# Two k products run together chunk by chunk, with the last maxima rounds between the chunks

## The chip, the cores and the metric

The kernel runs on one core of one Trainium2 chip. Everything is measured in microseconds of device time, from the start to the end of one execution. TensorE, VectorE (DVE), ScalarE (ACT), GpSimd (POOL) and SyncE (SP, which only issues transfers here) run their own instruction streams, and semaphores tie them together.

## What is computed

The input x holds 4 sequences of 2048 tokens of 512 numbers, the context 4 times 154 tokens. A layer norm, a cross attention and a gated channel mix (FFN) follow each other; cut to what matters:

```
xn = layernorm(x)
Q, K, V = xn @ Wq.T, ctx @ Wk.T, ctx @ Wv.T          # 16 heads of 32
x = x + tanh(g_xattn) * (softmax(Q K.T / sqrt(32)) V) @ Wo.T
x2 = layernorm(x)
xr = mu_r * x2 + (1 - mu_r) * x2_prev                # x2_prev: the token before
xk = mu_k * x2 + (1 - mu_k) * x2_prev
k = relu(xk @ W_k.T) ** 2
out = x + tanh(g_ffn) * sigmoid(xr @ W_r.T) * (k @ W_v.T)
```

## The kernel before

The 8192 tokens go in 16 blocks of 512. A product of two float32 matrices is made of three matmuls (high by high, high by low, low by high part), so one 128 x 512 piece of a product over 512 inputs takes 4 chunks of 3 matmuls. The step of block i (the function `step`, written once for each engine) computes the attention of block i and, between its parts, the FFN of block i - 1 and the queries of block i + 1. Step 0 has no FFN and transposes weights in its place; steps 1 to 14 are one hardware loop, step 15 and an epilogue with the last block's FFN stand behind it. So the FFN stands beside attention in fifteen steps.

The order on every engine is written out by hand, and each engine works strictly through its own list. What matters for the change is the start of a step:

- VectorE mixes the rows of k into the banks `o_bank` and `d_bank` (`mix_k`, line 865), ScalarE takes their high part (line 492) and VectorE their low part (`xk_low`, line 722). TensorE's k products (`ffn_k`, line 1176) wait for these low parts chunk by chunk. Output chunks 0 and 2 of k go to `g_bank` 0, chunks 1 and 3 to `g_bank` 1.
- Of the maxima of the scores (`maxima` on TensorE, line 1080; `reduce_max` on VectorE, line 813), there are six rounds. Rounds 0 to 3 lie in the step before. Round 4 has twelve small matmuls and four reduces, round 5 four and four. A round's matmuls wait for the reduces of the round before, as both use the four `s_bank`s.
- The maxima are transposed into `o_bank` (`maxima_transposed`, line 1007), and ScalarE copies them (`mT_copy`, line 492). The head scores of group 0 (`head_scores`, lines 1104 and 1108) need that copy for their last four matmuls. The next mixing for r (`mix_r(1)`, line 875) also waits for it, since it writes the same bank.
- Then ScalarE takes two exponentials from each bank (lines 598 and 599), VectorE the low half of the first (`p_low`, line 817), and the tail scores (`tail_scores`, line 1114) wait for that one, since they go to `s_bank` 0 again.
- VectorE takes the relu of each k chunk out of its bank (`k_relu`, line 842). GpSimd squares it (line 425), ScalarE and GpSimd split it (lines 492 and 429). k products 2 and 3 wait for the relus of 0 and 1, which free their banks. k product 1 waits for the copy of the fourth query out of `g_bank` 1 (`q_copy`, line 582).

In the kernel before, TensorE's list reads: k0 with round 4 ahead of its chunk 2; k1 with round 5 ahead of its chunk 1; the transpose of the maxima; k2 with the head scores ahead of its chunk 2; the tail scores; k3 and the first r product. VectorE's list behind the mixing reads: reduces of round 4, relu 0, reduces of round 5, relu 1, then `mix_r(1)`, `xr_low(0)`, `mix_r(2)`, `xr_low(1)`, `p_low(0)`.

Of the kernel before, what the change touches and what calls it, by code (L numbers as in the profile page):

```python
# [14 lines left out]
PRODUCTS = ((HI, HI), (HI, LO), (LO, HI))  # L15


def flamingo_block(nc, x, ctx_tokens, g_xattn, g_ffn, Wq, Wk, Wv, Wo, W_r, W_k, W_v, mu_r, mu_k, out):
# [8 lines left out]
    C = D // P  # L27
# [3 lines left out]
    BLOCKS = B * T // N  # L31
# [15 lines left out]
    with ExitStack() as ctx:  # L47
# [9 lines left out]
        WqT, WoT, WrT, WkT2, WvT2 = (sb(n, [P, 2, C, D], F32R) for n in ("WqT", "WoT", "WrT", "WkT2", "WvT2"))  # L57
# [6 lines left out]
        buf3 = sb("buf3", [P, 2, C, N], F32R)  # L64
# [107 lines left out]
        K_BANK = [g_bank[n] for n in (0, 1, 0, 1)]  # L172
# [547 lines left out]
        def _(dve):  # L720
# [115 lines left out]
            def k_relu(i, c):  # L836
                dve.wait_ge(k_done, i * C + c + 1)
                if c >= 2:
                    dve.wait_ge(k2_lo, i * C + c - 1)
                else:  # L840
                    later(dve, k2_lo, i * C)
                nc.vector.tensor_scalar(k2[c % 2], K_BANK[c][:, :], 0.0, None, ALU.max).then_inc(relu_ready, 1)  # L842
# [51 lines left out]

            def step(i, ffn, pre):
                reduce_max(i, 4)
                if ffn:
                    k_relu(i - 1, 0)
                else:
                    weight_low(late_units(0))  # L900
                reduce_max(i, 5)
                if ffn:
                    k_relu(i - 1, 1)
                    mix_r(i - 1, 1)
                    xr_low(i - 1, 0)
                    mix_r(i - 1, 2)
                    xr_low(i - 1, 1)
                p_low(i, 0, 0)
                if ffn:
                    mix_r(i - 1, 3)  # L910
                    xr_low(i - 1, 2)
                p_low(i, 0, 1)
                if ffn:
                    k_relu(i - 1, 2)
                    xr_low(i - 1, 3)
                p_low(i, 0, 2)
                p_low(i, 0, 3)
                if ffn:
                    k_relu(i - 1, 3)
                p_low(i, 0, 4)  # L920
                if not ffn:
                    weight_low(late_units(1))
                if pre:
                    moments1(i + 1, 0)
                    moments1(i + 1, 1)
                for g in range(1, G):
                    attend(i, g - 1)
                    p_low(i, g, 0)
                    p_low(i, g, 1)
                    if ffn and g == 2:  # L930
                        gated(i - 1, 1, pre)
                    if pre and g == 3:
                        xT_low(i + 1, 0)
                    p_low(i, g, 2)
                    p_low(i, g, 3)
                    p_low(i, g, 4)
                    if ffn and g != 2:
                        gated(i - 1, g - 1, pre)
                    if not ffn:
                        weight_low(late_units(1 + g))  # L940
                    if pre and g == 1:
                        moments1(i + 1, 2)
                        moments1(i + 1, 3)
                if pre:
                    for t in range(1, TT):
                        xT_low(i + 1, t)
                if not ffn:
                    weight_low(late_units(1 + G))
                attend(i, G - 1)
                if pre:  # L950
                    reduce_max(i + 1, 0)
                    reduce_max(i + 1, 1)
                    reduce_max(i + 1, 2)
                elif ffn:
                    gated(i - 1, TT - 1, pre)
                residual(i, 0, pre)
                if pre:
                    reduce_max(i + 1, 3, (0, 1))
                residual(i, 1, pre)
                if pre:  # L960
                    reduce_max(i + 1, 3, (2, 3))
                residual(i, 2, pre)
                residual(i, 3, pre)
                if pre and ffn:
                    gated(i - 1, TT - 1, pre)
                mix_k(i, 0)
                mix_k(i, 1)
                xk_low(i, 0)
                mix_k(i, 2)
                xk_low(i, 1)  # L970
                mix_k(i, 3)
                xk_low(i, 2)
                keep_carry(i)
                xk_low(i, 3)
                mix_r(i, 0)
# [19 lines left out]
        def _(pe):  # L995
# [14 lines left out]
            def cols(n):  # L1010
                return slice(P * n, P * n + P)
# [57 lines left out]
            def maxima(i, r):  # L1069

                if r == 0:
                    pe.wait_ge(k_loaded, 16 * K_LOADS * (i + 1))
                    later(pe, p_lo, i * SCORE_UNITS)
                    pe.wait_ge(xT_lo, (i + 1) * TT)
                else:
                    pe.wait_ge(reduced, i * MAX_UNITS + 4 * r)
                pe.wait_ge(q_hi, i * G + ROUNDS[r][-1][0] + 1)
                for n, (g, t) in enumerate(ROUNDS[r]):
                    for j in range(4):
                        ins = nc.tensor.matmul(s_bank[j][:, S * n:S * n + S], buf4[rows(j), HI, g, cols(t)], k_all[rows(j), g, :],  # L1080
                                               start=True, stop=True)
                        if n == len(ROUNDS[r]) - 1:
                            ins.then_inc(max_done, 1)
# [7 lines left out]
            def maxima_transposed(i):  # L1091
                pe.wait_ge(reduced, (i + 1) * MAX_UNITS)
                later(pe, x2_ready, i * TT - 1)
                transposed(mT_bank, [mm[:, t, :] for t in range(TT)]).then_inc(mT_done, 1)

            def head_scores(i, g):

                if g:
                    pe.wait_ge(p_lo, i * SCORE_UNITS + 5 * g)
                pe.wait_ge(q_lo, i * G + g + 1)  # L1100
                for k, (s, q) in enumerate(PRODUCTS):
                    for j in range(4):
                        keys = k_all[rows(j), g, 0:P] if s == HI else k_low[rows(j), g, :]
                        nc.tensor.matmul(s_bank[j][:, :], keys, buf4[rows(j), q, g, :], start=k == 0, stop=False)  # L1104
                if g == 0:
                    pe.wait_ge(mT_ready, i + 1)
                for j in range(4):
                    nc.tensor.matmul(s_bank[j][:, :], negsel[rows(j), g, DH * j:DH * j + 1].to_broadcast([DH, P]), mT[rows(j), :],  # L1108
                                     start=False, stop=True).then_inc(scores_done, 1)
# [51 lines left out]
                    pe.wait_ge(x2_ready, i * TT + t - 1)  # L1161
                transposed(x2_bank[t], [xn2[t % 2][:, cols(c)] for c in range(C)]).then_inc(x2_done, 1)

            def ffn_k(i, c, queries=True, before=None):


                if c >= 2:
                    pe.wait_ge(relu_ready, i * C + c - 1)
                elif c == 1 and queries:
                    pe.wait_ge(q_copied, (i + 1) * G + 4)  # L1170
                for e in range(C):
                    if before:
                        before(e)
                    pe.wait_ge(xk_lo, i * C + e + 1)
                    for n, (s, m) in enumerate(PRODUCTS):
                        ins = nc.tensor.matmul(K_BANK[c][:, :], WkT2[:, s, e, cols(c)], buf3[:, m, e, :],  # L1176
                                               start=(e, n) == (0, 0), stop=(e, n) == (C - 1, len(PRODUCTS) - 1))
                ins.then_inc(k_done, 1)

            def ffn_r(i, t):  # L1180

# [19 lines left out]
            def at(chunk, what):  # L1201
                return lambda c: what() if c == chunk else None
# [11 lines left out]

            def step(i, ffn, pre):
                if ffn:
                    ffn_k(i - 1, 0, before=at(2, lambda: maxima(i, 4)))
                    ffn_k(i - 1, 1, before=at(1, lambda: maxima(i, 5)))
                    maxima_transposed(i)
                    ffn_k(i - 1, 2, before=at(2, lambda: head_scores(i, 0)))  # L1220
                else:
                    maxima(i, 4)
                    weights_transposed(late_units(0))
                    maxima(i, 5)
                    maxima_transposed(i)
                    head_scores(i, 0)
                tail_scores(i, 0)
                if ffn:
                    ffn_k(i - 1, 3)
                    ffn_r(i - 1, 0)  # L1230
                else:
                    weights_transposed(late_units(1))
# [73 lines left out]
                step(i, True, True)  # L1306
            step(BLOCKS - 1, True, False)
            pe.wait_ge(x1_ready, BLOCKS * TT)
            for c in range(C):
                ffn_k(BLOCKS - 1, c, queries=False)  # L1310
            for t in (0, 1):
                ffn_r(BLOCKS - 1, t)
            for t in (0, 1):
# [25 lines left out]
```

## Time and profile before

| what | us |
|---|---|
| median of 3 runs (1563.97 to 1566.31) | 1564.04 |
| the profiled execution's own time | 1564.87 |
| its span, from the first to the last instruction | 1563.0 |
| TensorE busy (92%) | 1431.4 |
| VectorE busy (69%) | 1082.3 |
| ScalarE busy (50%) | 777.8 |
| GpSimd busy (39%) | 612.4 |
| mean granted TensorE clock | 0.951 |

Busy time is a sum of instruction times. The ends of matmuls are modelled and overlap the next one's start, so the distance from start to start is the better measure of a matmul's price. The granted clock is 1.00 for 2.4 GHz and 0.50 for 1.2 GHz. In a timeline an entry "x9" merges nine instructions; the bracket at its end tells how long the engine stood still before it and what ended that.

### The profile page before, as it was taken

What the parts mean: (1) busy time and instruction counts of PE and PEld (TensorE: products, weight loads), DVE (VectorE), ACT (ScalarE), POOL (GpSimd) and SP (SyncE); (2) the same over time, 40 slices, a digit from 0 to 9 for tenths busy, and PEclk for the clock granted to TensorE, in tenths of its full rate; (3) what the DMA queues carried; (4) which work ended last, traced back from release to release, by engine and by line L of the source; (5) the groups of instructions that cost most, each with busy time, mean ns of one, the idle gap of its engine ahead of it and who ended that gap; (6) DMA issues with size and microseconds to landing.
All of it is one profiled execution on the core that took longest, in us unless ns stands there. A gap on an engine that the chain in (4) does not pass through costs nothing.

```text
span 1563.0 us, 28266 instructions
## 1 busy us (share of the span) xinstructions
PE 1431.4 (92%) x9616; PEld 1041.5 (67%) x9616; DVE 1082.3 (69%) x1926; ACT 777.8 (50%) x1412; POOL 612.4 (39%) x807
## 2 busy tenths in 40 slices
PE   7866899998989899898989989898989989898978
PEld 6744667676767667676666757676766767666656
DVE  3465676867677686767777686767768676777652
ACT  3355273644637364554636455463736455463631
POOL 1111343535344442534344352534445253434333
PEclk9968899999999999998999999999999999999989
DMA  4422011121202012121101112120111212110100
GB/s 155 141 81 74 28 48 41 54 60 47 67 27 62 25 60 53 47 67 44 55 28 60 40 54 60 47 67 27 57 30 54 60 47 67 38 61 22 41 21 34
DMA packets 98364, 84.09 MB, mean 54 GB/s; under 512 B 49440, under 2 KB 62752, under 8 KB 98336
## 3 DMA queue, kind: packets, MB, share of 16 engines
q1 hardware_dynamic: 98336, 83.72, 17.9%
q8 instruction: 17, 0.28, 0.1%
q14 instruction: 11, 0.09, 0.0%
HBM read 58.79 MB, written 20.71 MB: 51 GB/s over the span
## 4 chain that ended last, share of the span: by engine, by line
PE 81%; DVE 10%; ACT 3%; issue 2%; POOL 1%; DMA 1%; SPq 1%; DVEq 0%; POOLq 0%; ACTq 0%
PE g_bank L1001 45%; PE g_bank L1176 9%; PE o_bank L1130 6%; PE s_bank L1104 4%; PE d_bank L1136 4%; PE s_bank L1114 3%; PE s_bank L1080 3%; DVE buf L722 2%; DVE o_bank L865 2%; PE o_bank L1007 2%; PE s_bank L1001 2%; DVE d_bank L865 2%; DVE mm L813 2%; PE d_bank L1007 1%; PE s_bank L1007 1%
## 5 line engine op out<-in xcount | busy, mean ns | idle before, releaser
L1176 PE MATMUL g_bank<-buf,WkT 128*128 128x512 f32 x768 | 236.1, 456 | 68.9 <-DVE buf L722 66.4
L813 DVE TENSOR_REDUCE mm<-s_bank 128x3 f32<-128x462 f32 (+1 forms) x384 | 198.7, 577 | 103.2 <-PE s_bank L1080 103.2
L817 DVE TENSOR_TENSOR pq<-s_bank,pq 128x512 f16<-128x512 f32 x320 | 218.4, 687 | 61.6 <-ACT s_bank L599 61.3
L598 ACT ACTIVATE pq<-s_bank 128x512 f16<-128x512 f32 x320 | 192.7, 602 | 108.1 <-PE s_bank L1108 108.0
L1176 PEld LDWEIGHTS g_bank<-buf,WkT 128*128 128x128 f32 x768 | 157.1, 217 | 123.6 <-DVE buf L722 76.8
L1001 PE MATMUL g_bank<-xnT,WqT 128*128 128x512 f32 x768 | 200.0, 407 | 3.6 <-DVE xnT L801 2.1
L599 ACT ACTIVATE s_bank<-s_bank 128x512 f32<-128x512 f32 x320 | 195.1, 610 | 0.0
L1001 PE MATMUL g_bank<-WvT,buf 128*128 128x512 f32 x768 | 192.3, 397 | 0.0
L1001 PE MATMUL g_bank<-WoT,buf 128*128 128x512 f32 x768 | 189.9, 397 | 0.0
L1001 PE MATMUL g_bank<-WrT,buf 128*128 128x512 f32 x768 | 188.9, 395 | 0.0
L433 POOL TENSOR_TENSOR buf<-place,buf 128x512 fp32r<-128x512 f32 x64 | 82.4, 1288 | 255.6 <-ACT buf L492 255.6
L1001 PEld LDWEIGHTS g_bank<-xnT,WqT 128*128 128x128 f32 x768 | 142.6, 192 | 40.5 <-DVE xnT L801 8.2
L1001 PEld LDWEIGHTS g_bank<-WrT,buf 128*128 128x128 f32 x768 | 141.8, 188 | 40.2 <-issue 11.0
L1001 PEld LDWEIGHTS g_bank<-WvT,buf 128*128 128x128 f32 x768 | 140.9, 188 | 34.2 <-issue 5.8
L1001 PEld LDWEIGHTS g_bank<-WoT,buf 128*128 128x128 f32 x768 | 140.7, 188 | 30.5
L429 POOL TENSOR_TENSOR buf<-place,buf 128x512 fp32r<-128x512 f32 x64 | 83.3, 1301 | 105.4 <-ACT buf L492 105.4
L492 ACT ACTIVATE buf<-place 128x512 fp32r<-128x512 f32 x128 | 81.4, 636 | 81.0 <-DVE place L834 65.8
L421 POOL TENSOR_TENSOR buf<-xa,buf 128x512 fp32r<-128x512 f32 x64 | 83.5, 1304 | 92.0 <-ACT xa L582 92.0
L441 POOL TENSOR_TENSOR x<-place,x 128x512 f32<-128x512 f32 x48 | 61.7, 1286 | 127.7 <-DVE place L847 127.7
L400 POOL TENSOR_TENSOR ve<-mv,eps 128x1 f32<-128x1 f32 x128 | 24.3, 190 | 216.3 <-DVE mv L767 216.3
L563 ACT ACTIVATE xa<-x,nb,rstd 128x512 f32<-128x512 f32 x64 | 52.0, 813 | 107.1 <-POOL nb L404 105.3
L425 POOL TENSOR_TENSOR place<-place 128x512 f32<-128x512 f32 x64 | 73.3, 1145 | 76.5 <-DVE place L842 76.5
(125 smaller groups left out, 2179.9 us busy)
## 6 DMA issues: line engine op xcount, KB each, us to landing
xa<-in_x SPq DMA_DIRECT2D x64, 256.0 KB, 2.7
x<-in_x SPq DMA_DIRECT2D x64, 256.0 KB, 2.7
out<-x SPq DMA_DIRECT2D x48, 256.0 KB, 2.0
k_all<-k_scratch SPq DMA_DIRECT2D x16, 256.0 KB, 2.8
k_low<-k_scratch SPq DMA_DIRECT2D x16, 256.0 KB, 2.9
v_main<-v_scratch SPq DMA_DIRECT2D x16, 256.0 KB, 2.8
place<-x SPq DMA_DIRECT2D x16, 256.0 KB, 2.3
out<-place SPq DMA_DIRECT2D x16, 256.0 KB, 2.0
```

Of the source, the lines that this page charges most:

```text
L421: nc.gpsimd.tensor_tensor(buf4[:, LO, g, :], q32[g], buf4[:, HI, g, :].bitcast(F32), ALU.subtract).then_inc(q_lo, 1)
L425: nc.gpsimd.tensor_tensor(k2[c % 2], k2[c % 2], k2[c % 2], ALU.mult).then_inc(k2_ready, 1)
L429: nc.gpsimd.tensor_tensor(buf1[:, LO, c, :], k2[c % 2], buf1[:, HI, c, :].bitcast(F32), ALU.subtract).then_inc(k2_lo, 1)
L433: nc.gpsimd.tensor_tensor(buf3[:, LO, g, :], attn32, buf3[:, HI, g, :].bitcast(F32), ALU.subtract).then_inc(attn_lo, 1)
L492: nc.scalar.activation(dst, src, ACT.Copy).then_inc(done, 1)
L598: nc.scalar.activation(pq[:, n, HI, :], bank[:, :], ACT.Exp, scale=SCALE).then_inc(p_hi, 1)
L599: nc.scalar.activation(bank[:, :], bank[:, :], ACT.Exp, scale=SCALE).then_inc(p_full, 1)
L813: nc.vector.reduce_max(maxima, scores, AX.X).then_inc(reduced, 1)
L817: nc.vector.tensor_tensor(pq[:, n, LO, :], score_bank[5 * g + n][:, :], pq[:, n, HI, :], ALU.subtract).then_inc(p_lo, 1)
L1001: ins = nc.tensor.matmul(dst, stationary(s, c), moving(m, c), start=(c, n) == (0, 0), stop=(c, n) == (chunks - 1, len(PRODUCTS) - 1))
L1130: nc.tensor.matmul(o_bank[rows(j), :], v, pq[:, 4 if n else j, q, :], start=(n, k) == (0, 0), stop=(n, k) == (1, 2))
L1176: ins = nc.tensor.matmul(K_BANK[c][:, :], WkT2[:, s, e, cols(c)], buf3[:, m, e, :], start=(e, n) == (0, 0), stop=(e, n) == (C - 1, len(PRO ...
```

## The change

TensorE now runs k0 and k1 together: for each of the four chunks of the mixed rows, three matmuls for output chunk 0 and three for output chunk 1. Round 4's maxima stand ahead of chunk 1 of this pair, round 5's ahead of chunk 3. The wait for the fourth query's copy, which stood ahead of k1, stands ahead of the pair. k2 follows, with the transpose of the maxima ahead of its chunk 2, then the head scores, and behind them directly the tail scores. On VectorE the relu of chunk 0 moves behind the reduces of round 5, so that both relus stand there. The epilogue takes the pair, k2 and k3 in the same way.

```diff
--- before.py
+++ after.py
@@ -894,12 +894,11 @@
 
             def step(i, ffn, pre):
                 reduce_max(i, 4)
-                if ffn:
-                    k_relu(i - 1, 0)
-                else:
+                if not ffn:
                     weight_low(late_units(0))
                 reduce_max(i, 5)
                 if ffn:
+                    k_relu(i - 1, 0)
                     k_relu(i - 1, 1)
                     mix_r(i - 1, 1)
                     xr_low(i - 1, 0)
@@ -1161,21 +1160,23 @@
                     pe.wait_ge(x2_ready, i * TT + t - 1)
                 transposed(x2_bank[t], [xn2[t % 2][:, cols(c)] for c in range(C)]).then_inc(x2_done, 1)
 
-            def ffn_k(i, c, queries=True, before=None):
-
-
-                if c >= 2:
-                    pe.wait_ge(relu_ready, i * C + c - 1)
-                elif c == 1 and queries:
+            def ffn_k(i, columns, queries=True, before=None):
+
+
+                if columns != (0, 1):
+                    pe.wait_ge(relu_ready, i * C + columns[0] - 1)
+                elif queries:
                     pe.wait_ge(q_copied, (i + 1) * G + 4)
                 for e in range(C):
                     if before:
                         before(e)
                     pe.wait_ge(xk_lo, i * C + e + 1)
-                    for n, (s, m) in enumerate(PRODUCTS):
-                        ins = nc.tensor.matmul(K_BANK[c][:, :], WkT2[:, s, e, cols(c)], buf3[:, m, e, :],
-                                               start=(e, n) == (0, 0), stop=(e, n) == (C - 1, len(PRODUCTS) - 1))
-                ins.then_inc(k_done, 1)
+                    for c in columns:
+                        for n, (s, m) in enumerate(PRODUCTS):
+                            ins = nc.tensor.matmul(K_BANK[c][:, :], WkT2[:, s, e, cols(c)], buf3[:, m, e, :],
+                                                   start=(e, n) == (0, 0), stop=(e, n) == (C - 1, len(PRODUCTS) - 1))
+                        if e == C - 1:
+                            ins.then_inc(k_done, 1)
 
             def ffn_r(i, t):
 
@@ -1214,10 +1215,9 @@
 
             def step(i, ffn, pre):
                 if ffn:
-                    ffn_k(i - 1, 0, before=at(2, lambda: maxima(i, 4)))
-                    ffn_k(i - 1, 1, before=at(1, lambda: maxima(i, 5)))
-                    maxima_transposed(i)
-                    ffn_k(i - 1, 2, before=at(2, lambda: head_scores(i, 0)))
+                    ffn_k(i - 1, (0, 1), before=lambda e: maxima(i, {1: 4, 3: 5}[e]) if e % 2 else None)
+                    ffn_k(i - 1, (2,), before=at(2, lambda: maxima_transposed(i)))
+                    head_scores(i, 0)
                 else:
                     maxima(i, 4)
                     weights_transposed(late_units(0))
@@ -1226,7 +1226,7 @@
                     head_scores(i, 0)
                 tail_scores(i, 0)
                 if ffn:
-                    ffn_k(i - 1, 3)
+                    ffn_k(i - 1, (3,))
                     ffn_r(i - 1, 0)
                 else:
                     weights_transposed(late_units(1))
@@ -1306,8 +1306,9 @@
                 step(i, True, True)
             step(BLOCKS - 1, True, False)
             pe.wait_ge(x1_ready, BLOCKS * TT)
-            for c in range(C):
-                ffn_k(BLOCKS - 1, c, queries=False)
+            ffn_k(BLOCKS - 1, (0, 1), queries=False)
+            ffn_k(BLOCKS - 1, (2,))
+            ffn_k(BLOCKS - 1, (3,))
             for t in (0, 1):
                 ffn_r(BLOCKS - 1, t)
             for t in (0, 1):
```

## Rows read from the trace of the kernel before

**Rows 1.** The page's part 1, and its part 4, the chain that ended last.
```profile
PE 1431.4 (92%) x9616; PEld 1041.5 (67%) x9616; DVE 1082.3 (69%) x1926; ACT 777.8 (50%) x1412; POOL 612.4 (39%) x807
...
PE 81%; DVE 10%; ACT 3%; issue 2%; POOL 1%; DMA 1%; SPq 1%; DVEq 0%; POOLq 0%; ACTq 0%
```

**Rows 2.** Waits: who waited for whom; us in total, times, longest.
```profile
PE g_bank L1176 <- DVE buf L722: 66.4, 18, 5.5
...
PE s_bank L1114 <- DVE pq L817: 12.6, 18, 2.8
...
PE s_bank L1080 <- DVE mm L813: 8.8, 9, 2.4
```

**Rows 3.** Timeline, TensorE: start, us, engine, line, operation, tiles, count, wait before.
```profile
454.60 3.10 PE L1176 MATMUL g_bank<-buf,WkT 128*128 128x512 f32 x6 [4.00 <-DVE buf L722]
...
461.88 0.34 PE L1080 MATMUL s_bank<-k_all,buf 32*128 32x154 f32 x4 [1.28 <-DVE mm L813]
462.15 2.34 PE L1176 MATMUL g_bank<-buf,WkT 128*128 128x512 f32 x9
464.33 0.60 PE L1007 MATMUL o_bank<-ident,mm 128*128 128x128 f32 x4
464.68 1.64 PE L1176 MATMUL g_bank<-buf,WkT 128*128 128x512 f32 x6
466.26 0.73 PE L1104 MATMUL s_bank<-buf,k_all 32*128 32x512 f32 x8
...
467.38 1.66 PE L1176 MATMUL g_bank<-buf,WkT 128*128 128x512 f32 x6
469.44 0.96 PE L1114 MATMUL s_bank<-buf,k_tail 128*128 128x512 f32 x3 [0.40 <-DVE pq L817]
```

**Rows 4.** Timeline of the same stretch, VectorE.
```profile
459.55 2.27 DVE L813 TENSOR_REDUCE mm<-s_bank 128x3 f32<-128x462 f32 x4
461.74 0.68 DVE L842 TENSOR_SCALAR place<-g_bank 128x512 f32<-128x512 f32 x1
462.34 0.98 DVE L813 TENSOR_REDUCE mm<-s_bank 128x1 f32<-128x154 f32 x4
...
465.60 0.76 DVE L875 SCALAR_TENSOR_TENSOR o_bank<-place,mu,x 128x512 f32<-128x512 f32 x1 [0.38 <-ACT mT L492]
...
468.70 0.68 DVE L817 TENSOR_TENSOR pq<-s_bank,pq 128x512 f16<-128x512 f32 x1
```

**Rows 5.** Timeline of the same stretch, ScalarE and GpSimd.
```profile
454.48 0.59 ACT L582 ACTIVATE xa<-g_bank 128x512 f32<-128x512 f32 x1
...
464.97 0.60 ACT L492 ACTIVATE mT<-o_bank 128x512 fp32r<-128x512 f32 x1 [4.69 <-PE o_bank L1007]
...
468.06 0.59 ACT L599 ACTIVATE s_bank<-s_bank 128x512 f32<-128x512 f32 x1
...
462.50 1.04 POOL L425 TENSOR_TENSOR place<-place 128x512 f32<-128x512 f32 x1 [4.27 <-DVE place L842]
```

**Rows 6.** Timeline, TensorE, in a block whose k products start at 722.60.
```profile
725.64 0.93 PE L1080 MATMUL s_bank<-k_all,buf 32*128 32x154 f32 x12
726.49 4.21 PE L1176 MATMUL g_bank<-buf,WkT 128*128 128x512 f32 x9
730.63 0.50 PE L1080 MATMUL s_bank<-k_all,buf 32*128 32x154 f32 x4
```

**Rows 7.** Windows: us, busy (count) of PE, PEld, DVE, ACT, POOL, clock, DMA, GB/s.
```profile
454.60:457.90 3.30, 3.30 (x10) 1.93 (x14) 3.15 (x5) 1.67 (x3) 2.99 (x3) 0.50 0.00 0
...
123.50:126.80 3.30, 3.23 (x11) 2.74 (x12) 2.02 (x4) 3.30 (x8) 1.28 (x1) 0.50 0.00 0
```

**Rows 8.** Timeline, TensorE, in the block before the loop and at the end.
```profile
123.56 1.65 PE L1114 MATMUL s_bank<-buf,k_tail 128*128 128x512 f32 x3 [2.06 <-DVE pq L817]
...
1529.21 7.36 PE L1176 MATMUL g_bank<-buf,WkT 128*128 128x512 f32 x24 [2.45 <-DVE place L842]
1536.41 5.60 PE L1001 MATMUL g_bank<-WrT,buf 128*128 128x512 f32 x24
```

## The prediction

> **What bounds the kernel now.** I read four views. The page's shares come first: TensorE is busy 92% of the span and holds 81% of the chain that ended last [rows 1]. So a change pays only where TensorE stands still or runs at its low clock. The sums of waits come second: TensorE's largest wait is for the mixed rows of k (66.4 us in 18 waits). Its second is for the low half of the first exponentials ahead of the tail scores (12.6 us in 18) [rows 2]. The third view is the order of time in one block. All fifteen blocks with an FFN part repeat it about 89.3 us apart (454.60, 543.94, and so on), and the change works in it. The fourth is the granted clock. The sum is made against the profiled execution, 1564.87 us (span 1563.0); the median of the runs is 0.83 lower.
>
> Take the block whose k products start at 454.60 after 4.00 us of standing still [rows 3]; times below count from there. TensorE does k0's first two chunks, the maxima of round 4, k0's rest and k1's first chunk. Then it waits 1.28 us until VectorE has reduced round 4, and does round 5 at 7.28. That start is VectorE's: its four reduces run 459.55 to 461.82 [rows 4], right behind its mixing. It is the same to 0.03 us in eleven of the fifteen blocks; in one it is 6.91, and in three where the low clock lasts it is 8.03 (as 722.60 to 730.63) [rows 6]. Then come the rest of k1 (nine matmuls, 2.18 us), the transpose of the maxima at 9.73, six matmuls of k2, the head scores (from 11.66 to 12.78), the last six matmuls of k2, and the tail scores at 14.84 after a wait of 0.40. The tail scores wait for VectorE's 0.68 at 468.70 to 469.38. This has two roads. ScalarE's second exponential ends at 468.65 [rows 5], 2.4 after the head scores began. VectorE can begin its own row only after mix_r(1) at 465.60, which waited for ScalarE's copy of the transposed maxima (464.97), and three operations behind it. Both roads begin at the transpose, and the tail scores come 5.11 us after it. **So the time of the transpose, not the amount of matmuls, sets the end of this stretch.**
>
> **The change, part by part.** No instruction is added or removed; matmuls, reduces and relus are as many as before. No DMA is issued or moved, and SP's queue keeps its order. What moves is TensorE's order and one relu on VectorE.
>
> *Start of the pair.* The wait for the fourth query copy stood ahead of k1 and now stands ahead of the first chunk. That copy ends at 455.07 (454.48 and 0.59) [rows 5], so the pair starts 0.47 late. This is covered: up to round 5 TensorE now has 18 matmuls and the twelve of round 4. At the high clock that is 18 times 0.242 (2.18 over nine) and 0.5, 4.9 us; from 0.47 it ends at 5.3, before the 7.28 that VectorE sets. At the low clock a matmul takes 0.46 (nine from 726.49 to 730.63) and the maxima 0.85 [rows 6]: 9.1 us, ending at 9.6. The clock is at half in the first 3.3 us of this block, [rows 7], and in the one of 722.60 nine of its matmuls still run at the slow pace [rows 6]. So the cost lies between 0 and 2.3 us a block; but before, too, the slow blocks lost 0.75 here, and the new order leaves fewer holes. I take 0.1.
>
> *Relus behind round 5.* Round 5 starts at 7.28 as now. VectorE is free, so it starts reducing some 0.3 later and is done with its 0.98 [rows 4] at 8.6. k0 ends at 8.43 (round 5's matmuls 0.27, three matmuls 0.73, and the 0.15 by which the last one's end trails), so relu 0 starts at about 8.6. From a relu's start to its waiter's there is 0.76 (461.74 to GpSimd's 462.50) [rows 4, 5]. So k2 starts at 9.33, where TensorE is through with k1 at 9.0: a new wait of 0.3. Bounds: none, if relu 0 were early, and 0.75 if nothing of it hid.
>
> *Transpose behind k2's first half.* Six matmuls, 1.45 us, bring it to 10.78. Before it was 9.73: **1.05 us later in each block**. Without the new wait it would be 0.72, with the whole 0.75 it would be 1.5. The Trainium skill (TensorE: Matmul & The Clock Gate, "Back-to-back issue gap") gives 216 ns a matmul of 512 columns at full clock. By it the six take 1.30 and the nine of before 1.94, which makes the difference 1.14; the trace has 242 ns, and the sum goes by that.
>
> *Head to tail.* The transpose's 0.35, six matmuls (1.58 up to the next, as 464.68 to 466.26) put the head scores 1.93 behind the transpose, exactly as before. They take 1.12. The tail scores stay 5.11 behind the transpose, so the wait ahead of them grows from 0.40 to 2.06, as the six matmuls that covered it are gone. Behind this wait stand k3, r0 and the first values, with all their readers, so it moves everything by 1.05. Nothing later takes that back: besides the two waits named, only the one for round 4's reduce recurs among TensorE's own (8.8 us in nine) [rows 2], and the next block's mixing is fed by TensorE's own transposes. GpSimd's square of k0 moves from 462.50 to about 464.0 and ends 1.04 later; it is needed once ScalarE has copied the maxima, about 1.5 us later. If that cover were gone the exponentials would queue behind it. The low part and chunks 2 and 3 of the relus shift with the rest.
>
> *Epilogue.* At 1529.21 k2 waits for relu 0 already [rows 8], which stands on VectorE behind seven operations of mixing in both orders: nothing.
>
> *The clock in the new wait.* The block before the loop has no k2 to cover the same place: the tail scores follow the head scores directly and start at 123.56 after a wait of 2.06, and from 123.5 to 126.8 the clock is 0.50, 1.2 instead of 2.4 GHz [rows 7, 8]. A wait of 2.45 at the end has the same consequence: 24 matmuls take 7.36 instead of 5.60 us, 1.76 more [rows 8]. Waits of 1.28 [rows 3] keep the clock high. The new wait is 2.06. The low stretches begin at varying places of the waits, so I do not take a fall in every block: bounds 0 and 15, taken 6, costing 10.5.
>
> Sum: 15 x (1.05 + 0.1) = 17.3, and 10.5: 1564.9 + 27.8 - 0.8 = 1591.9; I say 1591. The forecast's own range is 1585 to 1600 (3 to 10 falls).
>
> **Rivals.** *No falls:* what speaks for it is that every wait of a full TensorE under 1.3 us keeps the clock, and that tail scores and k3 follow densely. 1581.
>
> *Falls in every block:* every wait of 2 us and more that I found is followed by a low stretch. 17.3 + 26.4: 1608.
>
> *No change:* the shift is used up later in the block, at a place where TensorE waits for VectorE or ScalarE anyway and so would start when it starts now. It decides if such a wait of 1 us stands behind the tail scores; the sums show none that recurs [rows 2]. 1564, within 0.2%.
>
> *Faster:* the transpose is not what the tail scores hang on. If VectorE's mixing behind the copy left the first low half at its old distance from round 5, the path would be TensorE's own matmuls, and these have become shorter behind round 5: six instead of nine, 0.73 a block, 11 us in all, 1553. It decides when the wait ahead of the tail scores stays at 0.4. The 5.11 us that repeat in every block speak against it.
>
> *Evacuation:* the Trainium skill (Perfetto Trace Analysis, "Matmuls") wants independent groups in turn through the banks, so that one is emptied under the next one's matmuls. Here both banks are full at once, and the 0.3 is what that costs; it is in the sum.
>
> **How the numbers follow.** Forecast 0.56, no falls 0.30, falls everywhere 0.06, no change 0.04, faster 0.04. About 0.2% (3 us) can be told from no change. So slower 0.92, same 0.04, faster 0.04. The range reaches from the no-falls case with the smaller bound (15 x 0.85, 1577) up to 1603, some twelve falls. It leaves out the two small cases and the far end of the falls.
>
> **What would show it.** Round 5's maxima still 7.3 after the old start of k (6.8 after the new one); a wait of 0.3 ahead of k2 for a relu; the transpose 3.5 instead of 2.45 behind round 5; a wait of about 2 us ahead of the tail scores in each block, some followed by clock 0.50; total of that wait near 40 us. The prediction is wrong if that wait stays under 1 us, if the transpose comes no later, or if round 5 starts over 1 us late since the clock stays low.

## The result and the profile after

| | us |
|---|---|
| before, median of 4 runs (1563.97 to 1566.31) | 1565.11 |
| after, median of 4 runs (1593.67 to 1599.06) | 1597.03 |
| ratio, 95% interval | 1.0202 [1.0179, 1.0224] |
| the profiled execution after | 1599.06, span 1597.3 |

The change makes the kernel 2% slower, some 32 us. A second set of four runs of it, beside the last experiments, gave 1595.88 and 1.0207 [1.0188, 1.0227]. The profiled execution is 34.2 us longer than that of before, and this is the difference that I take apart below. (The forecast started from 1564.04, the median of the three runs known then.)

The page of the changed kernel, the same two lines as in [rows 1]:

```profile
PE 1434.9 (90%) x9616; PEld 1047.9 (66%) x9616; DVE 1084.6 (68%) x1926; ACT 776.3 (49%) x1412; POOL 612.4 (38%) x807
...
PE 80%; DVE 10%; ACT 4%; issue 3%; POOL 2%; SPq 1%; DMA 1%; DVEq 0%; POOLq 0%; ACTq 0%
```

TensorE has 3.5 us more of busy time and 34 us more of span. These sums do not price the clock. Matmuls at the low clock count as busy, and where TensorE would otherwise wait for VectorE the low clock costs nothing. In the kernel before, the blocks that start at 454.60 and 543.94 are 89.34 and 89.33 us long. The first is at the low clock until 3.4 behind its start and then waits 1.28 ahead of round 5. The second is at the low clock until 6.2 and waits 0.01. So the loss has to be read block by block. TensorE's own waits, the counterparts of [rows 2]:

```profile
PE g_bank L1176 <- ACT xa L582: 69.1, 15, 4.6
PE s_bank L1113 <- DVE pq L817: 35.6, 18, 2.1
...
PE s_bank L1079 <- DVE mm L813: 3.7, 6, 2.4
```

The wait ahead of the tail scores (L1113, L1114 before) grew from 12.6 to 35.6 us, by 23. The wait for the mixed rows at the start of k now ends with ScalarE's copy of the fourth query (L582). It is 4.61 in each block but the last (4.52) instead of 4.00: the copy ends at 737.15, and the pair starts 0.15 later.

One block in order of time, TensorE, the counterpart of [rows 3], with ScalarE's copy ahead of it. Its k products start at 737.30:

```profile
736.56 0.59 ACT L582 ACTIVATE xa<-g_bank 128x512 f32<-128x512 f32 x1
...
737.30 2.92 PE L1176 MATMUL g_bank<-buf,WkT 128*128 128x512 f32 x6 [4.61 <-ACT xa L582]
...
740.72 3.01 PE L1176 MATMUL g_bank<-buf,WkT 128*128 128x512 f32 x12
743.96 0.34 PE L1079 MATMUL s_bank<-k_all,buf 32*128 32x154 f32 x4 [0.23 <-DVE mm L813]
744.23 3.40 PE L1176 MATMUL g_bank<-buf,WkT 128*128 128x512 f32 x12
747.47 0.60 PE L1006 MATMUL o_bank<-ident,mm 128*128 128x128 f32 x4
747.83 1.64 PE L1176 MATMUL g_bank<-buf,WkT 128*128 128x512 f32 x6
749.40 0.74 PE L1103 MATMUL s_bank<-buf,k_all 32*128 32x512 f32 x8
...
750.20 0.39 PE L1107 MATMUL s_bank<-mT,negsel 32*128 32x512 f32 x4
752.58 0.97 PE L1113 MATMUL s_bank<-buf,k_tail 128*128 128x512 f32 x3 [1.99 <-DVE pq L817]
...
753.62 4.51 PE L1176 MATMUL g_bank<-buf,WkT 128*128 128x512 f32 x12
757.97 2.91 PE L1000 MATMUL g_bank<-WrT,buf 128*128 128x512 f32 x12
```

And VectorE in the same block, as in [rows 4]:

```profile
741.64 2.27 DVE L813 TENSOR_REDUCE mm<-s_bank 128x3 f32<-128x462 f32 x4
744.33 0.99 DVE L813 TENSOR_REDUCE mm<-s_bank 128x1 f32<-128x154 f32 x4 [0.43 <-PE s_bank L1079]
745.24 1.36 DVE L842 TENSOR_SCALAR place<-g_bank 128x512 f32<-128x512 f32 x2
748.74 0.76 DVE L875 SCALAR_TENSOR_TENSOR o_bank<-place,mu,x 128x512 f32<-128x512 f32 x1 [2.14 <-ACT mT L492]
...
751.85 0.68 DVE L817 TENSOR_TENSOR pq<-s_bank,pq 128x512 f16<-128x512 f32 x1
```

The new start of k lies 0.61 later than the old one against the mixing, so 0.61 is added to set these times beside the old ones ("on the old scale"). Round 5 is at 6.66 (7.27 on the old scale, 7.28 before). Behind it twelve matmuls take 3.24 instead of the 2.91 that twelve cost at 0.242: that includes a wait of 0.33 for relu 0, which VectorE starts at 745.24. The transpose is at 10.17, on the old scale 10.78 instead of 9.73. The tail scores are at 15.28, or 15.89 instead of 14.84, 1.05 later, after a wait of 1.99 instead of 0.40. Then k3's twelve matmuls take 4.35 us up to r0 (753.62 to 757.97). In the kernel before they take 2.74:

```profile
470.47 2.91 PE L1176 MATMUL g_bank<-buf,WkT 128*128 128x512 f32 x12
473.21 2.88 PE L1001 MATMUL g_bank<-WrT,buf 128*128 128x512 f32 x12
```

The granted clock tells why. The windows are of the changed kernel (us; busy time and count of five engines; clock; DMA):

```profile
737.50:740.30 2.80, 2.80 (x10) 1.76 (x10) 2.70 (x5) 1.19 (x2) 2.80 (x2) 0.50 0.00 0
740.70:750.00 9.30, 8.96 (x54) 6.51 (x54) 6.67 (x14) 2.19 (x4) 1.73 (x2) 1.00 0.34 113
754.20:757.30 3.10, 3.10 (x9) 2.43 (x8) 2.88 (x5) 3.10 (x8) 2.02 (x2) 0.50 0.70 243
```

The clock is at half at the start of k, as before, and once more right behind the new wait, from 754.2 to 757.3. In the profiled execution such a stretch (a fall, below) follows the wait in nine of the fifteen blocks.

### The profile page after: what moved, and what is told of

Its sections match the earlier page's. It is cut to its first block, busy times and chain, and to the rows that moved or that the text cites. A ratio compares the mean times of both kernels' runs of the same rounds, so it can differ in the third digit from the quotient of the medians.

```text
span 1597.3 us, 28266 instructions
## 1 busy us (share of the span) xinstructions
PE 1434.9 (90%) x9616; PEld 1047.9 (66%) x9616; DVE 1084.6 (68%) x1926; ACT 776.3 (49%) x1412; POOL 612.4 (38%) x807
## 4 chain that ended last, share of the span: by engine, by line
PE 80%; DVE 10%; ACT 4%; issue 3%; POOL 2%; SPq 1%; DMA 1%; DVEq 0%; POOLq 0%; ACTq 0%
PE g_bank L1000 43%; PE g_bank L1176 9%; PE o_bank L1129 6%; PE s_bank L1103 4%; PE d_bank L1135 4%; PE s_bank L1113 3%; PE s_bank L1079 3%; DVE mm L813 2%; DVE o_bank L865 2%; DVE buf L722 2%; PE o_bank L1006 2%; PE s_bank L1000 2%; DVE d_bank L865 2%; PE d_bank L1006 1%; PE s_bank L1006 1%
## 5 line engine op out<-in xcount | busy, mean ns | idle before, releaser
L1176 PE MATMUL g_bank<-buf,WkT 128*128 128x512 f32 x768 | 239.4, 463 | 77.7 <-ACT xa L582 69.1
L1176 PEld LDWEIGHTS g_bank<-buf,WkT 128*128 128x128 f32 x768 | 165.6, 225 | 129.5 <-DVE buf L722 70.6
L1000 PEld LDWEIGHTS g_bank<-WvT,buf 128*128 128x128 f32 x768 | 140.9, 188 | 35.6 <-issue 5.8
```

What stands on the lines that cost most here:

```text
L1000: ins = nc.tensor.matmul(dst, stationary(s, c), moving(m, c), start=(c, n) == (0, 0), stop=(c, n) == (chunks - 1, len(PRODUCTS) - 1))
```

## The experiments

All times are medians beside runs of the kernel before on the same chip (1564.8 to 1566.2). Eleven kernels ran, and the changed one once more. Dead matmuls below are extra ones whose results are overwritten before anything reads them. The time of the first k products varies between the profiled executions, from 181.2 to 188.5 us, though no edit touches what stands ahead of them. So single profiled times can differ by some us that the experiment did not cause.

### The transpose first

```diff
-                    ffn_k(i - 1, (2,), before=at(2, lambda: maxima_transposed(i)))
-                    head_scores(i, 0)
+                    maxima_transposed(i)
+                    ffn_k(i - 1, (2,), before=at(2, lambda: head_scores(i, 0)))
```

> The changed kernel with one edit on TensorE: the transpose of the maxima stands right behind the pair, ahead of k2, and the head scores stand inside k2 as before. The pair and both relus behind round 5 stay. My theory (the time of the transpose sets the end of the stretch): the transpose comes about 0.7 us earlier than in the kernel before instead of about 1 us later, the wait ahead of the tail scores falls to 0.4 to 0.7, no low clock follows it, and the kernel is faster than the one before: 1565 - 15 x 0.73 = 1554, up to 1558 if the clock at the start of k costs more. The rival (the pair with its late start and the relus behind round 5 are what costs): still slower than before, 1575 or more.

Measured: 1554.69, ratio 0.9939 [0.992, 0.9957]. TensorE in a block whose k products start at 536.72:

```profile
543.37 0.34 PE L1079 MATMUL s_bank<-k_all,buf 32*128 32x154 f32 x4
...
545.13 0.60 PE L1006 MATMUL o_bank<-ident,mm 128*128 128x128 f32 x4
...
547.06 0.74 PE L1103 MATMUL s_bank<-buf,k_all 32*128 32x512 f32 x8
...
550.42 0.96 PE L1113 MATMUL s_bank<-buf,k_tail 128*128 128x512 f32 x3 [0.58 <-DVE pq L817]
```

The transpose is at 8.41 (9.02 on the old scale, 0.71 early), the wait 0.58, and no low clock follows it in any block. One edit turns 2% slower into 0.6% faster, so the pair and the late relus are not what costs. The tail scores come 5.29 behind the transpose instead of 5.11. VectorE shows the reason:

```profile
546.40 0.76 DVE L875 SCALAR_TENSOR_TENSOR o_bank<-place,mu,x 128x512 f32<-128x512 f32 x1 [0.38 <-ACT mT L492]
...
547.92 1.12 DVE L875 SCALAR_TENSOR_TENSOR d_bank<-xa,mu,x 128x512 f32<-128x512 f32 x1
...
549.69 0.68 DVE L817 TENSOR_TENSOR pq<-s_bank,pq 128x512 f16<-128x512 f32 x1
```

mix_r(2) takes 1.12 instead of 0.94, and the low half starts at 549.69, right behind VectorE's mixing.

### k3 over the wait

```diff
-                tail_scores(i, 0)
                 if ffn:
-                    ffn_k(i - 1, (3,))
+                    ffn_k(i - 1, (3,), before=at(2, lambda: tail_scores(i, 0)))
                     ffn_r(i - 1, 0)
                 else:
+                    tail_scores(i, 0)
```

> The changed kernel, but the tail scores stand in the middle of k3 instead of ahead of it, so six matmuls lie in the wait; the transpose stays behind k2's first half. Theory (a late transpose costs through the uncovered wait, and the low clock follows that wait): TensorE catches up 1.45 us in the wait, the values then hang on ScalarE's exponentials, which are 1.0 late and had 0.9 in hand: between 0 and +0.4 us a block, 1565 to 1571, and no low clock behind the head scores. Rival (the late transpose itself shifts everything, covered or not): 1565 + 15 x 1.08 = 1581.

Measured: 1579.03, ratio 1.0095 [1.0075, 1.0115]. That is near the rival's number. TensorE in one of its blocks:

```profile
833.16 1.67 PE L1176 MATMUL g_bank<-buf,WkT 128*128 128x512 f32 x6
835.21 0.96 PE L1113 MATMUL s_bank<-buf,k_tail 128*128 128x512 f32 x3 [0.37 <-DVE pq L817]
...
838.67 2.97 PE L1000 MATMUL g_bank<-WrT,buf 128*128 128x512 f32 x12 [0.88 <-DVE buf L722]
```

The wait ahead of the tail scores is down to 0.37 and the clock stays high, but r0 now stands still for 0.88 until VectorE's last low part of the r mixing (L722). That mixing begins with mix_r(1), behind the copy of the transposed maxima. This wait occurs in all fifteen blocks, 13.1 us in all. So a late transpose is carried on VectorE's road as well, and filling the wait on TensorE takes back the clock but hardly the shift. My theory, 1565 to 1571, is out.

### Six dead matmuls in the wait

```diff
                     head_scores(i, 0)
+                    pe.wait_ge(relu_ready, (i - 1) * C + 2)
+                    for e in range(2):
+                        for n, (s, m) in enumerate(PRODUCTS):
+                            nc.tensor.matmul(K_BANK[3][:, :], WkT2[:, s, e, cols(3)], buf3[:, m, e, :],
+                                             start=n == 0, stop=n == len(PRODUCTS) - 1)
```

> The changed kernel with six extra matmuls behind the head scores that write bank 1 of g_bank and are overwritten by k3 (dead work; what is computed stays). They fill 1.45 of the 2.05 us wait and delay nothing. Theory (9 low stretches behind that wait cost 1.6 us each): they go, and the time falls from 1597 to 1580 to 1585. Rival (the low clock costs nothing, as ScalarE and VectorE set the pace there): 1595 to 1599.

Measured: 1587.93, ratio 1.0141 [1.0116, 1.0166], 8 to 9 us less than the changed kernel. It misses my range from above, and the rival's from below.

```profile
748.35 1.66 PE L1224 MATMUL g_bank<-buf,WkT 128*128 128x512 f32 x6
750.40 0.97 PE L1113 MATMUL s_bank<-buf,k_tail 128*128 128x512 f32 x3 [0.40 <-DVE pq L817]
...
751.44 2.89 PE L1176 MATMUL g_bank<-buf,WkT 128*128 128x512 f32 x12
754.17 2.88 PE L1000 MATMUL g_bank<-WrT,buf 128*128 128x512 f32 x12
```

The dead matmuls stand at 748.35, and the tail scores wait 0.40 more. k3's twelve up to r0 take 2.73, at the high clock, in this and all blocks. So the falls were worth 8 to 9 us of the median here (1595.9 and 1597.0 against 1587.9). The theory wanted 12 to 17. The two profiled executions, 10.6 us apart, show the rest: no block has a fall, which gives back 14.4. But the low clock at the start of k lies worse, round 5 is 8.0 in sum behind 6.66 instead of 6.3. And the first k products start 2.1 later (188.54 for 186.45). 14.4 less 1.7 less 2.1 is 10.6.

### Relu 0 alone

VectorE's edit on the kernel before, TensorE's order untouched.

```diff
-                if ffn:
-                    k_relu(i - 1, 0)
-                else:
+                if not ffn:
                     weight_low(late_units(0))
                 reduce_max(i, 5)
                 if ffn:
+                    k_relu(i - 1, 0)
```

> The kernel before with VectorE's edit alone: relu 0 behind the reduces of round 5, TensorE's order untouched. Theory: k2 needs the relu only at 10.08 after the start of k and gets it at 9.4, so nothing changes: 1565, within 2 us. Rival (relu 0 late delays GpSimd's and ScalarE's split and so the exponentials): over 0.3 us a block, 1570 or more.

Measured: 1564.30, ratio 0.9995 [0.9984, 1.0006]: nothing.

### The late transpose alone

On the kernel before, with k0 and k1 one after the other:

```diff
-                    maxima_transposed(i)
-                    ffn_k(i - 1, 2, before=at(2, lambda: head_scores(i, 0)))
+                    ffn_k(i - 1, 2, before=at(2, lambda: maxima_transposed(i)))
+                    head_scores(i, 0)
```

> The kernel before with one part of the change alone: the transpose of the maxima stands ahead of k2's third chunk and the head scores behind k2; k0 and k1 one after the other as before, relu 0 between the rounds. Theory (the late transpose with its uncovered wait is the whole loss, and the pair takes a little of it back): six matmuls later, 15 x 1.45 = 22, and 6 to 9 falls of the clock at 1.6: 1597 to 1601. Rival (the pair costs as well, by its late start and the wait for relu 0): less than the whole change, 1580 to 1590.

Measured: 1605.24, ratio 1.0257 [1.0232, 1.0282]: more than the whole change, and above the range that I gave. A block whose k products start at 923.49:

```profile
931.05 3.70 PE L1176 MATMUL g_bank<-buf,WkT 128*128 128x512 f32 x15
934.59 0.60 PE L1007 MATMUL o_bank<-ident,mm 128*128 128x128 f32 x4
...
939.70 1.65 PE L1114 MATMUL s_bank<-buf,k_tail 128*128 128x512 f32 x3 [1.99 <-DVE pq L817]
```

The transpose is at 11.10, 1.37 later than the 9.73 of before, and the tail scores at 16.21, 1.37 later than 14.84. A low clock follows the wait in all fifteen blocks, not in 6 to 9. The rival is out: the pair does not cost, it gives 0.3 us a block back (the shift is 1.37 here and 1.05 with the pair). Fifteen times 1.37 and 1.5 are 43 us, for 41 between the profiled executions: my range had too few falls.

### The head scores late

The changed kernel with only this:

```diff
-                    ffn_k(i - 1, (2,), before=at(2, lambda: maxima_transposed(i)))
+                    maxima_transposed(i)
+                    ffn_k(i - 1, (2,))
                     head_scores(i, 0)
```

> The changed kernel with the transpose ahead of all of k2, but the head scores still behind k2, directly ahead of the tail scores. Theory as I put it before (the time of the transpose sets the tail scores, 5.11 later): 1554, as with the transpose first. Rival (a second road, from the head scores over two exponentials, 3.18 to 3.36 us long, takes over, and its wait is uncovered): the tail scores 0.6 later than in the kernel before, 15 x 0.6 = 9, and falls of the clock in half of the blocks, 12: 1580 to 1588.

Measured: 1602.80, ratio 1.0245 [1.0228, 1.0262]. Both numbers are too low, but the place is the rival's:

```profile
743.52 0.60 PE L1006 MATMUL o_bank<-ident,mm 128*128 128x128 f32 x4
...
746.80 0.74 PE L1103 MATMUL s_bank<-buf,k_all 32*128 32x512 f32 x8
...
749.98 1.65 PE L1113 MATMUL s_bank<-buf,k_tail 128*128 128x512 f32 x3 [1.97 <-DVE pq L817]
```

The transpose is at 9.05 (9.66 on the old scale), as early as before the change, and yet the tail scores come 6.46 behind it. They come 3.18 behind the head scores, as in the kernel before. That is the second road, over two exponentials. So the sentence that the transpose's time alone sets the stretch is false in general. In the kernels where the head scores stand 1.93 behind the transpose, the two roads end nearly together: before, ScalarE's second exponential ends at 468.65 and VectorE begins its row at 468.70 [rows 4, 5]. The wait is 1.97, and a low clock follows it in thirteen of fifteen blocks, where I had counted on half. Those blocks are 92.1 to 92.2 long, 2.8 over the 89.33 of before. The head scores give 0.7 of that, the low clock at the start of k 0.65 (round 5 at 7.3 instead of 6.66), and the fall 1.5.

### An earlier start of the pair

```diff
-                elif queries:
-                    pe.wait_ge(q_copied, (i + 1) * G + 4)
                 for e in range(C):
...
                     for c in columns:
+                        if (e, c) == (0, 1) and queries:
+                            pe.wait_ge(q_copied, (i + 1) * G + 4)
```

> The changed kernel, but the wait for the fourth query's copy stands ahead of k1's first chunk inside the pair instead of ahead of the whole pair, so k0's first three matmuls can start some 0.6 us earlier. Theory A (the late start adds to the work at low clock that pushes round 5 behind 6.66 us in seven of fifteen blocks, 6.3 us in all in the profile): about half of it comes back, 1591 to 1595. Theory B (round 5 is set by VectorE and the start is covered): no change from the changed kernel, 1595 to 1599.

Measured: 1594.31 (1585.53 to 1595.39), ratio 1.0168 [1.0135, 1.02]. Its time overlaps with that of the changed kernel, and one of its runs is 8 us under the others, so the median does not decide. The profile tells more:

```profile
732.95 2.73 PE L1176 MATMUL g_bank<-buf,WkT 128*128 128x512 f32 x6 [4.00 <-DVE buf L722]
...
740.22 0.34 PE L1079 MATMUL s_bank<-k_all,buf 32*128 32x154 f32 x4 [0.68 <-DVE mm L813]
```

The pair starts 4.00 behind, not 4.61. Round 5 is at 7.27, and TensorE even waits 0.68 for it. Over the fifteen blocks round 5 lies 1.9 us in sum behind 7.27; in the changed kernel it lies 6.3 in sum behind its 6.66. So the late start does matter where the clock is low, by some 4 us. Ten low stretches behind the new wait in this profile, instead of nine, took part of it back.

### Both waits filled

The six dead matmuls of above, and ahead of the pair:

```diff
+                    for n in range(16):
+                        nc.tensor.matmul(g_bank[0][:, :], WqT[:, HI, n % C, cols(0)], xnT[:, HI, n % C, :], start=True, stop=True)
                     ffn_k(i - 1, (0, 1), before=lambda e: maxima(i, {1: 4, 3: 5}[e]) if e % 2 else None)
```

> The changed kernel with dead matmuls in both waits: the six behind the head scores of the earlier run, and sixteen ahead of the pair that fill 3.9 of the 4.6 us wait for the mixed rows (they write g_bank 0, which k0 overwrites; what is computed stays). Theory (three terms: 1.08 us a block from the order, 1.5 for each fall behind the head scores, and up to 1.1 a block from the low clock at the start of k): only the first is left, 16 us less the 2 that the kernel before itself loses to the low clock there: 1578 to 1582. Rival (the low clock at the start is covered; the order costs more than 1.08): as with the six alone, 1585 to 1589.

Measured: 1581.69, ratio 1.0112 [1.0094, 1.013], in the range of the theory. A block whose pair starts at 730.75:

```profile
725.97 3.79 PE L1219 MATMUL g_bank<-xnT,WqT 128*128 128x512 f32 x16
730.75 1.65 PE L1176 MATMUL g_bank<-buf,WkT 128*128 128x512 f32 x6 [1.00 <-ACT xa L582]
...
737.43 0.34 PE L1079 MATMUL s_bank<-k_all,buf 32*128 32x154 f32 x4 [1.56 <-DVE mm L813]
...
746.07 0.96 PE L1113 MATMUL s_bank<-buf,k_tail 128*128 128x512 f32 x3 [0.42 <-DVE pq L817]
...
749.85 0.39 PE L1000 MATMUL g_bank<-WrT,buf 128*128 128x512 f32 x1
```

The sixteen take 3.79, and the pair behind them starts at the high clock. Then TensorE waits 1.56 for round 4's reduces, round 5 is at 6.68, and r0 comes 19.10 behind the start of the pair. In the block of 737.30 above it takes 20.67. Its profile has two low stretches more, both behind the wait for round 4's reduces. Their blocks are 91.86 and 91.63 long, while ten of the others are 90.41 to 90.45. What is left is 16.9 us over the kernel before. Less 2.6 for these two, and with the 1.9 that the kernel before itself loses at the start of k, the order comes to 16.2, or 1.08 a block.

### The low half of the exponentials ahead of the mixing

The kernel with the transpose first, on VectorE:

```diff
                     mix_r(i - 1, 2)
-                    xr_low(i - 1, 1)
                 p_low(i, 0, 0)
                 if ffn:
+                    xr_low(i - 1, 1)
                     mix_r(i - 1, 3)
```

> The kernel with the transpose first (1554.7 measured), and on VectorE the first low half of the exponentials ahead of xr_low(1) instead of behind it. Theory (there VectorE's mixing road ends last, at 549.69 against ScalarE's 549.45): the tail scores 0.2 us earlier in each block, 3 us in all, 1551 to 1553. Rival (the r products then wait for xr_low(3), as they did where k3 covered the wait): no gain or a loss, 1554 to 1560.

Measured: 1558.17, ratio 0.9954 [0.9937, 0.997], over the 1554.69 without the edit. VectorE and then TensorE in a block whose k products start at 544.64:

```profile
557.41 0.69 DVE L817 TENSOR_TENSOR pq<-s_bank,pq 128x512 f16<-128x512 f32 x1 [0.44 <-ACT s_bank L599]
...
561.33 0.68 DVE L722 TENSOR_TENSOR buf<-o_bank,buf 128x512 fp32r<-128x512 f32 x1
```

```profile
558.16 0.96 PE L1113 MATMUL s_bank<-buf,k_tail 128*128 128x512 f32 x3 [0.39 <-DVE pq L817]
...
559.19 2.90 PE L1176 MATMUL g_bank<-buf,WkT 128*128 128x512 f32 x12
562.16 2.06 PE L1000 MATMUL g_bank<-WrT,buf 128*128 128x512 f32 x8
```

The tail scores are at 13.52 instead of 13.70, the 0.2 that was expected. But k3's twelve matmuls up to r0 take 2.97 instead of 2.72, because r0 needs xr_low(3). VectorE ends it at 562.01, 0.15 ahead of r0. The blocks are 0.12 longer, and three of them lose up to 1.1 to a long low clock at the start. The rival is right.

### Two more on the version with the transpose first

With the earlier start of the pair (the diff of that section on top of the transpose first):

> The kernel with the transpose first (1554.7 measured), and the wait for the fourth query's copy only ahead of k1's first chunk. Theory (its profile has round 5 at VectorE's time in all blocks but two, so the start of the pair is covered): 1553 to 1556, no difference. Rival (the start counts): 15 x 0.6 = 9 less, 1546.

Measured: 1555.80, ratio 0.9949 [0.9931, 0.9966]. No difference, as the theory says.

With the sixteen dead matmuls ahead of the pair (likewise):

> The kernel with the transpose first and the sixteen dead matmuls ahead of the pair. Theory: the clock stays high there, but round 5 is VectorE's, so nothing but the two late blocks and the spread comes back: 1552 to 1555. Rival (the low clock costs there too): 1545 or less.

Measured: 1556.27, ratio 0.9947 [0.993, 0.9965]. Nothing comes back, and it is 1 us above the range of the theory; the rival, 1545 or less, is out. TensorE at full clock only waits longer for round 4's reduces (1.59 in a block). In two blocks a low stretch follows that wait, and these are 1.4 us longer than the others (90.29 against 88.86 in one). So the dead matmuls bring a small cost of their own there.

The changed kernel once more:

> The changed kernel once more, on the chip of the three others: 1594 to 1599 if the four runs so far hold; the number of low stretches behind the head scores (9 in the first profile) may differ.

Measured: 1595.88 (1595.63 to 1598.13). Its profile has eight low stretches behind the new wait instead of nine, and partly in other blocks than in the first profile.

## Why the prediction held, and where its terms were off

Forecast: 1591, range 1577 to 1603, slower with 0.92. Measured: 1597.0. Both sums against the profiled execution of before:

| term | forecast | measured | from |
|---|---|---|---|
| order (transpose later) | 15 x 1.05 = 15.8 | 15 x 1.08 = 16.2 | distance of two k starts in the one block with no low clock behind the wait and a short one at the start, 90.41, against 89.33 |
| low clock at the start of k | 15 x 0.1 = 1.5 | 4.4 | round 5 behind 6.66, 6.3 in sum, less the 1.9 by which it lies behind 7.28 in the kernel before |
| falls in the new wait | 6 x 1.75 = 10.5 | 9 x 1.6 = 14.4 | k3's twelve matmuls to r0, 4.35 against 2.74 |
| sum | 27.8 | 35.0; profile 34.2 | |

**The order.** Right nearly to the hundredth: transpose forecast at 10.78, measured at 10.78 on the old scale. The wait behind round 5 was put at 0.3 and is 0.33. The wait ahead of the tail scores was put at 2.06, near 40 us in all, and is 1.99 and 35.6. The tail scores come 1.05 later. The run with both waits filled leaves this term nearly alone: 16.9, and 16.2 once the low stretches of both kernels are set off. The run with the transpose first removes it and brings the gain of the faster rival, 10 us of its 11. So that rival had a true mechanism in it, the shorter work behind round 5, which the change itself gave away by putting six matmuls ahead of the transpose.

**One sentence of it was too strong:** "the time of the transpose, not the amount of matmuls, sets the end of this stretch". I had named two roads and said that both begin at the transpose. The one over ScalarE begins at the head scores. With these late it takes over, 3.18 behind them. In the change the transpose and the head scores moved together, so the forecast did not depend on the difference. And "behind this wait stand k3, r0 and the first values" told only TensorE's side. VectorE's mixing for r hangs on the same copy, and r0 on that, which is why k3 in the wait did not help (1579 for an expected 1565 to 1571).

**The start of the pair.** The term that was mis-sized: 1.5 us forecast, 4.4 measured. The copy's end at 0.47 is right, but the pair starts 0.61 late; the 0.15 from the copy's end to the waiter was left out. And 0.1 a block for the low clock was a choice between bounds of 0 and 2.3, not a reading. The earlier start shows that these two meet: the same 18 matmuls, begun 0.6 sooner, bring round 5's lateness from 6.3 to 1.9 us. Its cost in the median stays open within some 4 us, since the number of falls changes from run to run.

**The falls.** Their mechanism was right, and the price (1.76 forecast, 1.6 measured). Their number was a guess, 6 for 9. The dead matmuls in the wait remove them and 8 to 9 us of the median; the profiled executions agree with 14.4 for the falls, once the start of k and the time ahead of the first block are set off (see there). What decides how many blocks have one was not settled. The number is 8 and 9 in two profiles of the changed kernel, 10 with the earlier start, 13 with the head scores late and 15 with the late transpose alone, and all these waits are 2.0 us. The Trainium skill (TensorE: Matmul & The Clock Gate, "What's actually happening") describes the low clock as the default state, which activity lifts. The traces agree as far as they go: no low stretch begins in, or right behind, a wait that dead matmuls filled (the clock is 1.00 there).

**The evacuation.** The rule of the Trainium skill (Perfetto Trace Analysis, "Matmuls") speaks for turns between the banks. The measured price of filling both at once is the 0.33, and it vanishes when the transpose stands between the pair and k2: then TensorE has no wait there. The order of the rest decided, not this.

## What to carry to other kernels

When work is moved to fill one wait, look for what it is put ahead of. Here six matmuls of k2 came to stand ahead of the transpose and the head scores instead of behind them. The chain over ScalarE and VectorE began 1.05 us later, and TensorE waited 1.6 us more for its end, with its clock falling behind that wait in half of the blocks. Matmuls of k3 in the wait won back the clock but not the shift (1579). The transpose ahead of all of k2, with the head scores in its middle, won back everything (1555). Put small instructions that feed a long chain on other engines (here a transpose of 0.35 us and the head scores) as early as their inputs allow, and bulk matmuls behind them. A wait of 2 us on TensorE can cost nearly twice its length, as the clock may fall behind it.

## What the runs showed of the hardware

With TensorE at the high clock before it, a wait of 2.0 us was followed by a stretch at 1.2 GHz in 8 to 15 of 15 blocks, depending on the kernel. Each cost 1.6 us. A wait of 1.6 us was followed by one in 2 of the 14 blocks that have it, in each of two kernels (both waits filled, and the transpose first with the sixteen). Waits of 1.2 to 1.3 us were followed by none in the four blocks of the kernel before that have them, waits of 0.4 to 0.6 us by none. Dead matmuls in the wait kept the clock at 2.4 GHz and made the kernel 8 to 9 us faster. Dead matmuls ahead of the pair kept it too, but gave nothing in the kernel with the transpose first, where VectorE sets the pace (1556.3 against 1554.7). The best kernel found is that one, 0.6% faster than before and 2.7% faster than the changed one.
